# Second attention of a two-layer block: softmax sums taken from the mixing products, inverted as short rows and spread by transfers, with the step put in another order

## The reference, cut to what matters

```python
q = (layernorm(x) @ Wq).reshape(16, 128, 32, 16)          # 16 batches, 128 rows, 32 heads of 16
k, v = split(ctx @ Wkv)                                   # the same shape
q, k = rope(q, pos), rope(k, pos)
w = softmax(einsum('bqhd,bkhd->bhqk', q, k) / 4, axis=-1)
x = x + einsum('bhqk,bkhd->bqhd', w, v).reshape(16, 128, 512) @ Wout + bout
```

## Time and profile before

| what | value |
|---|---|
| runs | 1961.34, 1964.09, 1964.13 us, median 1964.09 |
| profiled execution, its own time | 1962.21 us |
| its span, first to last instruction | 1960.4 us |
| PE busy | 1910.0 us (97%) |
| DVE busy | 1320.1 us (67%) |
| ACT, POOL busy | 735.2 us (37%), 558.9 us (29%) |
| the attention's steps | about 1092 to 1414 us of the span |

### The profile page before, as it was taken

The page is one execution under the profiler, slowest core; times in us unless marked ns, Lnnn a source line. Parts: engine busy times, 40 slices in busy tenths (PEclk is TensorE's granted clock), DMA queues, the critical chain, the costliest instruction groups (busy, mean ns, idle before and its releaser), DMA issues. The chain is left out here.

```text
span 1960.4 us, 35844 instructions
## 1 busy us (share of the span) xinstructions
PE 1910.0 (97%) x13296; PEld 1539.0 (79%) x13296; DVE 1320.1 (67%) x2493; ACT 735.2 (37%) x2275; POOL 558.9 (29%) x705
## 2 busy tenths in 40 slices
PE   6999999999999999999999899999999999999999
PEld 4788888778888878888888677777688888888887
DVE  6666666765665655334253699998768877888786
ACT  5545545655555532211121444444423222122211
POOL 3323322322224326211021434343210222322231
PEclk9999999999999999999999999999999999999999
DMA  6553333544355433111022200000121545664554
GB/s 202 130 157 79 92 72 84 148 104 109 96 133 141 115 106 100 50 42 54 11 79 86 71 20 21 24 19 27 46 92 55 193 152 198 204 198 164 195 169 157
DMA packets 157014, 205.62 MB, mean 105 GB/s; under 512 B 23536, under 2 KB 111600, under 8 KB 156912
## 3 DMA queue, kind: packets, MB, share of 16 engines
q1 hardware_dynamic: 133200, 117.26, 21.7%
q0 software_dynamic: 23712, 87.04, 13.5%
HBM read 136.61 MB, written 17.30 MB: 79 GB/s over the span
## 5 line engine op out<-in xcount | busy, mean ns | idle before, releaser
L2388 POOL DMA_INDIRECT m_ring<-in_table,m_row x128 | 126.0, 985 | 371.0 <-DVE l_x_all L2501 271.0
L48 PE MATMUL four_banks<-l_yT_hi,m_hi 128*128 128x512 f32 x512 | 199.4, 389 | 0.0
L48 PE MATMUL four_banks<-l_yT_lo,m_hi 128*128 128x512 f32 x512 | 199.2, 389 | 0.0
L534 ACT ACTIVATE prob<-four_banks,mx,rms 128x128 f32<-128x128 f32 x256 | 121.8, 581 | 166.8 <-DVE mx L673 166.8
L1150 DVE TENSOR_SCALAR f_relu<-bank,f_b 128x512 f32<-128x512 f32 x64 | 48.0, 750 | 166.5 <-ACT f_h_hi L1093 166.4
L1093 ACT ACTIVATE f_h_hi<-bank,f_b 128x512 fp32r<-128x512 f32 x64 | 44.1, 690 | 261.4 <-PE bank L48 261.4
L336 POOL TENSOR_TENSOR rms<-ssq,constants 128x4 f32<-128x4 f32 x128 | 25.6, 200 | 395.3 <-ACT junk_k L522 278.6
L339 POOL TENSOR_TENSOR rms<-rms,constants 128x4 f32<-128x4 f32 x128 | 130.2, 1017 | 10.0
L48 PEld LDWEIGHTS four_banks<-l_yT_hi,m_hi 128*128 128x128 f32 x512 | 96.1, 188 | 20.1 <-issue 0.2
L48 PEld LDWEIGHTS four_banks<-l_yT_lo,m_hi 128*128 128x128 f32 x512 | 96.1, 188 | 20.0
L2365 ACT ACTIVATE m_act_of<-m_dot,l_ln_y 128x2 f32<-128x2 f32 x64 | 18.9, 296 | 237.4 <-DVE m_junk L2491 237.4
(11 more groups left out here) (314 smaller groups left out, 5287.2 us busy)
## 6 DMA issues: line engine op xcount, KB each, us to landing
qkT<-blocks SPq DMA_DIRECT2D x256, 128.0 KB, 2.7
pT_sb<-dealt SPq DMA_DIRECT2D x256, 64.0 KB, 2.1
f_stage<-in_w POOLq DMA_DIRECT2D x14, 512.0 KB, 4.5
f_x_in<-x SPq DMA_DIRECT2D x18, 256.0 KB, 3.2
ctx_in<-in_ctxT SPq DMA_DIRECT2D x32, 128.0 KB, 2.6
x_in<-in_x SPq DMA_DIRECT2D x16, 256.0 KB, 3.2
x<-xres SPq DMA_DIRECT2D x16, 256.0 KB, 2.8
x<-l_x_all SPq DMA_DIRECT2D x16, 256.0 KB, 2.1
```

The lines of the kernel that those rows point to most:

```text
L48: mm = pe.matmul(out, st, mv, start=first and n == 0, stop=last and n == len(terms) - 1)
L534: a = act.activation(prob[g][:, j, :].rearrange("q (b a) -> q a b", b=4), scores, ACT.Exp, bias=mx[g][:, 1, j:j + 1], scale=rms[g][:, 0, j ...
L2388: pool.indirect_dma_start(ring[slot][:], None, table, bass.IndirectOffsetOnAxis(ap=row[:, tile_of(g), k:k + 1], axis=0)).then_inc(S[f"got{ ...
```

## The change

`v_sb` is filled with ones where it held zeros: each head has its 16 value columns first and 16 columns of ones behind. A mixing matmul of one head then gives 16 rows of output and 16 equal rows of sums, and nothing is accumulated over f: f = 1 goes to bank 6, f = 0 to bank 7. `sum_up` is gone. ACT copies both banks out (`o_in`). SP then issues, for every tile, nine transfers (`move_outputs`): two that take one row of sums of each head to a small tile `sums` of 128x32, four that bring the odd heads' outputs from `rden` into `o_sb`, two that write the inverted sums to a DRAM tensor `inverses`, and one that reads them back into all 128 rows of `rden`, each row of it 16 times. `invert` works on 128x32; `normalise` reads SBUF alone. The steps of all five engines are in another order.

```diff
-    ones = sb("ones", [P, 3 * D], F32)
+    sums = sb("sums", [P, 32], F32)
+    evacuated = (o_sb, rden)
+        def move_outputs(s):
+            for f in range(2):
+                sp.wait_ge(*at(f"o_in{1 - f}", s))
+                sp.dma_start(sums[64 * (1 - f):64 * (2 - f), :], evacuated[1 - f][D:P:PAD, :]).then_inc(S["o_moved"], 16)
+            sp.wait_ge(S["o_moved"], 144 * s + 32)
+            for j in range(4):
+                sp.dma_start(o_sb[PAD * j + D:PAD * (j + 1), :], rden[PAD * j:PAD * j + D, :]).then_inc(S["o_moved"], 16)
+            sp.wait_ge(*at("inv_ready", s))
+            for f in range(2):
+                sp.dma_start(inverses[:, f, :], sums[64 * f:64 * (f + 1), :]).then_inc(S["o_moved"], 16)
+            sp.wait_ge(S["o_moved"], 144 * s + 128)
+            sp.dma_start(rden[:], inverses.rearrange("j f x -> (j f) x").unsqueeze(1).to_broadcast([8, D, DM])
+                         ).then_inc(S["o_moved"], 16)
         def step(s):
+            if there(s - 1):
+                move_outputs(s - 1)
             if there(s + 2):
                 load_ctx(sp, s + 2)
+            if there(s + 1):
+                move_maxima(s + 1, 0)
             if there(s - 1):
                 store(s - 1)
...
             if there(s + 1):
-                move_maxima(s + 1, 0)
                 move_maxima(s + 1, 1)
     def mix(pe, s):
         pe.wait_ge(*at("v_copied", s))
-        for t in range(4):
-            for f in range(2):
-                for j in range(4):
-                    mm = pe.matmul(bank[7][PAD * j:PAD * (j + 1), t * P:(t + 1) * P], v_sb[:, 8 * t + 2 * j + f, :],
-                                   probT[f][:, j, t, :], start=f == 0, stop=f == 1)
-        mm.then_inc(S["mixed"], 1)
...
+        for f in (1, 0):
+            if f == 0 and not there(s + 1):
+                pe.wait_ge(*at("o_in0", s - 1))
+            for t in range(4):
+                for j in range(4):
+                    mm = pe.matmul(bank[(7, 6)[f]][PAD * j:PAD * (j + 1), t * P:(t + 1) * P], v_sb[:, 8 * t + 2 * j + f, :],
+                                   probT[f][:, j, t, :], start=True, stop=True)
+            mm.then_inc(S[f"mixed{f}"], 1)
+    def o_in(act, s, f):
+        act.wait_ge(*at(f"mixed{f}", s))
+        if there(s - 1):
+            act.wait_ge(*at(("oT_lo", "o_ready")[f], s - 1))
+        act.activation(evacuated[f][:], bank[(7, 6)[f]][:], ACT.Copy).then_inc(S[f"o_in{f}"], 1)
     def invert(dve, s):
-        dve.wait_ge(*at("summed", s))
-        dve.reciprocal(rden[:], bank[6][:]).then_inc(S["rden_ready"], 1)
+        dve.wait_ge(S["o_moved"], 144 * s + 32)
+        dve.reciprocal(sums[:], sums[:]).then_inc(S["inv_ready"], 1)
     def normalise(dve, s):
-        dve.wait_ge(*at("rden_ready", s))
-        dve.wait_ge(*at("mixed", s))
...
-        dve.tensor_tensor(o_sb[:], bank[7][:], rden[:], ALU.mult).then_inc(S["o_ready"], 1)
+        dve.wait_ge(S["o_moved"], 144 * (s + 1))
+        dve.tensor_tensor(o_sb[:], o_sb[:], rden[:], ALU.mult).then_inc(S["o_ready"], 1)
```

More of the change, by code:

```diff
@@ L1212, in l0_ffn, with l1_attention @@
     return over, ahead, {"sync": sync, "gpsimd": gpsimd, "tensor": tensor, "scalar": scalar, "vector": vector}
[L1215 removed]
+def l1_attention(place, sem, bank, score_banks, ident, over, x2, ctxT, pos, wq, wkv, wo, bo, wr, keys_in, peaks, inverses, x3):
     H, D, PAD = 32, 16, 32
@@ L1469, in step @@
             if there(s + 1):
-                split_ctx(pool, s + 1)
-            if there(s + 1) and not (isinstance(s, int) and s == 0):
-                by_cosine(pool, s + 1, 0)
-            if there(s - 1):
-                split_o(pool, s - 1)
-            if there(s + 1):
                 by_cosine(pool, s + 1, 1)
@@ L1603, in sum_up @@
             pe.wait_ge(*at("k_copied", s + 1))
-        for f in range(2):
-            for j in range(4):
-                mm = pe.matmul(bank[6][PAD * j:PAD * (j + 1), :], ones[:, D * (1 - f):D * (3 - f)],
-                               probT[f][:, j, :, :].rearrange("p t q -> p (t q)"), start=f == 0, stop=f == 1)
-        mm.then_inc(S["summed"], 1)
+        for f in (1, 0):
[6 more added lines that the diff above has]
+            mm.then_inc(S[f"mixed{f}"], 1)
     def output(pe, s):
@@ L1683, in step @@
         def step(s):
+            last = isinstance(s, int) and s == NB - 1
             if there(s + 1) and not (isinstance(s, int) and s == 0):
@@ L1687, in step @@
                 score_shifted(pe, s, 0)
-            if there(s - 1):
-                output(pe, s - 1)
             if there(s + 1):
@@ L1693, in step @@
                 turn_y(pe, s - 2)
-            if isinstance(s, int) and s == NB - 1:
+            if last:
                 turn_y(pe, SHORT)
+            if there(s + 2):
+                queries(pe, s + 2)
+            if there(s + 1):
+                turn_k(pe, s + 1, 0)
             if there(s):
                 score_shifted(pe, s, 1)
-            if isinstance(s, int) and s == NB - 1:
+            if last:
                 turn_y(pe, SHORT + 1)
@@ L1701, in step @@
             if there(s + 1):
-                turn_k(pe, s + 1, 0)
-            no_queries = isinstance(s, int) and s == NB - 2
-            if there(s + 2):
-                queries(pe, s + 2)
-            if no_queries:
+                turn_k(pe, s + 1, 1)
                 turn_q(pe, s + 1, 1)
-                turn_k(pe, s + 1, 1)
+                values(pe, s + 1)
+                score(pe, s + 1, 0)
+            if there(s - 1):
+                output(pe, s - 1)
             if there(s + 1):
-                score(pe, s + 1, 0)
-                if not no_queries:
-                    turn_k(pe, s + 1, 1)
-            if there(s):
-                sum_up(pe, s)
-            if there(s + 1):
-                if not no_queries:
-                    turn_q(pe, s + 1, 1)
-                values(pe, s + 1)
                 score(pe, s + 1, 1)
@@ L1836, in step @@
         def step(s):
-            if there(s - 1):
-                o_hi(act, s - 1)
             if isinstance(s, int) and s == NB - 1:
@@ L1851, in step @@
                 y_hi(act, SHORT)
+            if there(s + 2):
+                copy_qk(act, s + 2, 0)
+            if there(s + 1):
+                turned_in(act, s + 1, 1, 0)
+                turned_in(act, s + 1, 1, 1)
             if there(s):
@@ L1856, in step @@
             if there(s + 1):
-                turned_in(act, s + 1, 1, 0)
-                turned_in(act, s + 1, 1, 1)
-            if there(s + 2):
-                copy_qk(act, s + 2, 0)
-            if there(s + 1):
                 turned_in(act, s + 1, 0, 1)
+            if there(s - 1):
+                o_hi(act, s - 1)
             if there(s + 2):
                 ctx_hi(act, s + 2)
+            if there(s):
+                o_in(act, s, 1)
+                o_in(act, s, 0)
             if there(s + 1):
@@ L2074, in step @@
                 rope(dve, s + 1, 0)
+            if there(s + 2):
+                x_lo(dve, s + 2)
+            if there(s - 2):
+                layer_norm_y(dve, s - 2)
             if there(s + 1) and not (isinstance(s, int) and s == 0):
                 by_sine(dve, s + 1, 1)
-            if there(s + 2):
-                x_lo(dve, s + 2)
+            if there(s - 1):
+                invert(dve, s - 1)
             if there(s + 1):
                 rope(dve, s + 1, 1)
+            if turned_here(s - 2):
+                y_lo(dve, s - 2)
+            if isinstance(s, int) and s == NB - 1:
+                y_lo(dve, SHORT)
             if there(s + 2):
                 copy_cosines(dve, s + 2)
-            if there(s - 1):
-                add_y(dve, s - 1)
-                dve.wait_ge(*at("y_added", s - 1))
             if there(s + 3):
@@ L2122, in vector @@
         chain[0] = 0
+        invert(dve, NB - 1)
+        normalise(dve, NB - 1)
+        layer_norm_y(dve, NB - 2)
         ahead["vector"](dve, 1)
```

82 lines of the change are left out of this document (41 added, 41 removed).

## The result

| | kernel before | changed kernel |
|---|---|---|
| median | 1963.54 us (4 runs) | **2029.72 us** (4 runs, 2029.25 to 2033.95) |
| ratio | | 1.0344, 95% interval 1.0329 to 1.0358 |
| span of the profiled execution | 1960.4 us | 2027.6 us |
| PE, DVE busy | 1910.0, 1320.1 us | 1917.2, 1257.3 us |
| mean granted clock | 0.995 | 0.977 |

The change costs 66 us, where 14 were forecast (1978 us, range 1957 to 2000). The sign was right; the time lies outside the range. PE's busy time went up, although 256 matmuls are gone, and its mean clock fell: this is the first thing to follow.

What follows compares the result with a forecast made beforehand. PE bounded the kernel before; a path closing through SP would bound the changed one: 11.30 us plus 9.4 of transfers, 20.70 us a step. Eleven periods +3.2 us and the rest, together +15.2, gave 1978 us, range 1957 to 2000.

Steps and rivals of the forecast that it cites:

- The circle through SP: In each step, every output waits by way of SP for the output before it; 20.70 us a step, 0.29 more than before.
- (d): Last of the nine transfers, reading the inverses into 128 rows, 256 KB: 2.9 us plus 0.05 to hand over, 2.95 us.
- (D): Rival: the read of the inverses is spread over half of the engines, 3.2 us; total 1982 us, chance 0.15.
- (b): SP's four issues of the moved outputs at 0.42 us each: 1.7 us, between 1.4 and 2.6.
- The output product: First term of a step, on PE: taken at 3.02 us, as in the kernel before.
- The sine products: DVE's sine products of q, put ahead of the second maxima: 0.75 us of each step.
- The ends: Last steps of the stage: into step 14 +5.4 us, into step 15 +4.3, the last output +2.8.
- C: The nine transfers of one step, with three landings in series: 9.4 us, low ends 7.4, high ends 11.6.
- Rival (B): The transfers are slow: sums and inverses take 2.6 us, the step's transfers 10.9; total 2000 us, chance 0.13.
- Rival (A): The transfers are quick, near 8.0 us a step, and PE's gain shows; total 1956 us, chance 0.2.
- (C): Rival: DVE's late head of the step delays PE's `turn_y` by 2.1 us; 20 us a step, 1964 us, chance 0.1.

Runs made afterwards that it cites:

- e7_order16: Changed kernel with the read of the inverses in another order of dimensions, 16 groups of 8 rows instead of 8 rows 16 times; 2022.54 us, ratio 1.0298.
- e1_fill: Changed kernel with ten useless filler matmuls in PE's gap ahead of each output product of tiles 0 to 13; 2015.74 us, ratio 1.0265.
- e16_sine_first: Changed kernel with the sine products of q put ahead of `add_y` on DVE; 2026.98 us, ratio 1.0319.
- e5: Changed kernel with all nine transfers left out and `normalise` waiting only for ACT's copies; 1962.92 us, ratio 0.9997.
- e8: Changed kernel with sums sent ahead of the second maxima and a masked merge on DVE replacing the four moves; 1980.81 us, ratio 1.0084.
- e2_read_rows: Changed kernel with the last transfer reading 128 different rows instead of 8 rows 16 times each; 2001.0 us, ratio 1.0181.
- e3_no_moves: Changed kernel without the four transfers that move the odd heads' outputs; 1984.05 us, ratio 1.0095.
- e6_early_sums: Changed kernel with the two transfers of sums issued ahead of the second maxima transfer; 1989.81 us, ratio 1.0128.

## Why the prediction was wrong, point by point

1. **What bounds the changed kernel: right.** The circle through SP closed as forecast and set every step: the gap lies in front of L58 (2.7 us, forecast 2.4), DVE idles 6.1 us for `inverses`, and the first transfer of sums is issued right behind the branch. Five of its ten terms came within 0.1 us; four of those five had a row of their own in the trace before.
2. **The read, (d): mis-sized.** 4.07 us, forecast 2.95, and above the end of 3.2 that I kept. The rows that I took as nearest were loads of 128 or more distinct rows. (D) named one cause and put 0.3 us on it; e7_order16 puts it at 0.5, less than half of the difference. The prediction also says that no row has a transfer with so few rows on one side; the read of the maxima, with 4 as its outer dimension, is one (1.99 us), but its 8 KB tell nothing of 256.
3. **The issues, (b): mis-sized.** 0.65 us each, forecast 0.42, at the end of the bound (2.6). I took a mean over issues of unlike forms.
4. **The output product: the term that failed, held for constant when it wasn't.** I copied 3.02 us from a stage without gaps and, in the same text, forecast a gap of 2.4 us in front of it. The product after the gap took 4.34 us (4.45 in the mean of eleven), most of it at a granted clock of 0.51; e1_fill shows that the gap is the cause. By e1_fill this is 14 us of the 66, and no part of the prediction named it. Of the 3.37 us by which the step was forecast too short, the product makes 1.3, the read 1.1, the issues 0.9.
5. **The sine products: right,** 0.68 us on the circle where 0.75 was forecast. What they are worth is less, 0.5 us a step by e16_sine_first, since the score on PE runs beside them; that leaves the forecast's sum as it is.
6. **The ends.** Into step 14 +9.8 instead of +5.4, into 15 +7.7 instead of +4.3: C's 2.2 us more and the clock each time (0.76 in the window from 1420 to 1448 us, 0.85 from 1448 to 1471). The weight loads also hold back SP's own issues: four moves took 3.66 us there instead of 2.57.
7. **Rival (B)** came nearest with 2000 us and for the wrong reason: sums and inverses landed in 1.80 us each, not 2.6. (Nor was the queue full where the 2.7 came from: the DMA share from 295 to 345 us of the kernel before is 0.36.) **Rival (A)** fails, since C is 11.6 and not 8.0. **(C)** holds in part as soon as the path is short: e5's step is the 20 us that it gave, with waits of 0.80 and 0.16 us at that place and not 2.1, and in e8 the rotated keys are late by 0.37. `normalise`, which now reads SBUF twice, wasn't held up: 0.69 us, with POOL idle.
8. **The range.** C came out at 11.59 us; its stated high end was 11.6. That end was added up wrongly: the high ends of its four parts make 12.3. The range stopped at C = 10.9 and took no account of the clock. C at its high end alone would have taken it to about 2010, and the clock's 1.3 us a step from there to about 2030.

## What to carry to other kernels

When a forecast puts an idle gap in front of a PE product, price the product behind it at the slower clock as well as at the full one: here, of eleven gaps of 2.3 to 2.9 us, ten had some 3 us of matmuls or more behind them at half the clock; of eleven of 0.9 to 1.4 us (e2_read_rows), five had; of those under 0.8 us in e3_no_moves and e6_early_sums none had. When a change takes 1.85 us from the busiest engine and adds a chain through the transfer queue, close the circle and add up its terms, then ask of each transfer whether the row used for it has the same form (distinct rows, outer dimension) and not only the same size. And before paying for such a path, run the new order without it: e5_no_path would have shown that this order had nothing to win.
